# A transformer block on one core: batch passes replaced by a 16-slot pipeline, Q and K stacked by 24 transfers per group

## What is computed

```python
def attn(x, Wqkv, Wo):              # H = 16 heads of HD = 32
    q, k, v = heads(x @ Wqkv)
    scores = einsum('bhqd,bhkd->bhqk', q, k) * HD ** -0.5
    a = softmax(where(causal, scores, -1e9))
    return merge(einsum('bhqk,bhkd->bhqd', a, v)) @ Wo

def ffn(x, w1, w3, w2):             # HIDDEN = 1365
    w1q, w3q, w2q = [clip(round(w / mean(abs(w))), -1, 1) * mean(abs(w)) for w in (w1, w3, w2)]
    return (silu(x @ w1q.T) * (x @ w3q.T)) @ w2q.T

x = x + attn(layernorm(x), Wqkv, Wo)
x = x + ffn(layernorm(x), w1, w3, w2)
```

## Time and profile before

| | |
|---|---|
| time, median of 3 runs | 727.8 us (727.48 to 729.08) |
| span of the profiled execution, first to last instruction | 727.0 us |
| TensorE (PE) busy | 630.4 us, 87% |
| TensorE weight loads | 300.6 us, 41% |
| VectorE (DVE) busy | 436.0 us, 60% |
| ScalarE (ACT) busy | 335.2 us, 46% |
| GpSimd (POOL) busy | 136.4 us, 19% |
| mean granted TensorE clock | 0.941 of full speed |
| chain that ended last | PE 64%, DVE 17%, ACT 11%, issue 5% |

### The profile page before, as it was taken

How to read it: one execution, slowest core, us unless ns; L and a number is a source line. 1 busy time by engine, 2 the same in 40 slices (tenths; PEclk the granted TensorE clock), 3 DMA queues, 4 the chain that set the end, 5 groups by cost and what they waited for, 6 DMA issues and landing times.

```text
span 727.0 us, 10700 instructions
## 1 busy us (share of the span) xinstructions
PE 630.4 (87%) x3892; PEld 300.6 (41%) x3892; DVE 436.0 (60%) x816; ACT 335.2 (46%) x551; POOL 136.4 (19%) x205
## 2 busy tenths in 40 slices
PE   2695687677988999999979999999979999997998
PEld 1142333333444444444444444444434544443443
DVE  7767767974655668634575777535556775244431
ACT  2556756852345585511456555501557645202330
POOL 2000012311100233410001225401002233211330
PEclk9997888667999999999999999999999999997999
DMA  8061121300020000011100000021000000120001
GB/s 330 16 227 58 48 79 54 116 1 1 1 73 16 16 16 1 1 59 60 52 23 17 16 16 1 1 76 40 15 16 16 1 16 1 44 72 1 0 1 59
DMA packets 13930, 30.22 MB, mean 42 GB/s; under 512 B 2442, under 2 KB 2442, under 8 KB 13876
## 3 DMA queue, kind: packets, MB, share of 16 engines
q1 hardware_dynamic: 13876, 29.50, 12.8%
HBM read 20.97 MB, written 4.19 MB: 35 GB/s over the span
## 4 chain that ended last, share of the span: by engine, by line
PE 64%; DVE 17%; ACT 11%; issue 5%; DMA 2%; SPq 0%; POOL 0%; DVEq 0%; ACTq 0%; POOLq 0%
PE work L999 25%; PE work L1139 11%; PE work L1030 10%; PE sum_bank L1102 6%; PE o_bank L1102 4%; PE prob_bank L1083 3%; PE score_bank L1056 3%; ACT k_stack L625 3%; DVE block_max L829 3%; ACT probs L642 2%; DVE inv_sum L844 1%; ACT late L684 1%; DMA late<-in_L_ffn_w 1%; ACT late L657 1%; ACT q_stack L625 1%
## 5 line engine op out<-in xcount | busy, mean ns | idle before, releaser
L999 PE MATMUL work<-late,w_ternary 128*128 128x512 f16 (+1 forms) x704 | 168.3, 390 | 9.6 <-DVE late L864 8.1
L829 DVE TENSOR_REDUCE block_max<-score_bank 128x4 f32<-128x512 f32 x160 | 102.8, 684 | 52.3 <-PE score_bank L1058 52.2
L999 PEld LDWEIGHTS work<-late,w_ternary 128*128 128x128 f16 (+1 forms) x704 | 69.9, 102 | 90.6 <-DVE late L864 14.2
L642 ACT ACTIVATE probs<-prob_bank,scalars 128x512 f32<-128x512 f32 x160 | 100.6, 681 | 7.0 <-PE prob_bank L1083 6.0
L568 POOL TENSOR_TENSOR late<-late 128x512 f16<-128x512 f32 (+1 forms) x44 | 51.0, 1159 | 208.5 <-ACT late L663 208.5
L1139 PE MATMUL work<-w_ternary,late 128*128 128x512 f16 (+1 forms) x352 | 77.2, 379 | 0.0
L864 DVE SCALAR_TENSOR_TENSOR late<-late,work 128x512 f32<-128x512 f32 (+1 forms) x44 | 30.3, 688 | 68.7 <-ACT late L657 68.4
L1056 PE MATMUL score_bank<-k_stack,q_stack 96*128 96x512 f16 (+3 forms) x256 | 62.7, 310 | 9.3 <-DVE block_max L829 8.4
L844 DVE RECIPROCAL inv_sum<-sum_bank 128x512 f32<-128x512 f32 x16 | 53.7, 3358 | 21.5 <-PE sum_bank L1102 21.5
L1030 PE MATMUL work<-xt_hi,wqkv_hi 128*128 128x512 f16 x128 | 51.5, 402 | 17.0 <-DVE wqkv_lo L778 10.4
L647 ACT ACTIVATE ot_hi<-o_sb 128x512 f16<-128x512 f32 x16 | 10.1, 630 | 121.0 <-DVE o_sb L850 121.0
(11 more groups left out here) (104 smaller groups left out, 911.3 us busy)
## 6 DMA issues: line engine op xcount, KB each, us to landing
late<-in_L_ffn_w SPq DMA_DIRECT2D x6, 768.0 KB, 6.5
x_res<-in_L_attn_x SPq DMA_DIRECT2D x16, 256.0 KB, 2.7
out_y<-x_res SPq DMA_DIRECT2D x16, 256.0 KB, 2.0
late<-in_L_attn_Wqkv SPq DMA_DIRECT2D x4, 768.0 KB, 8.9
xn<-in_L_attn_x SPq DMA_DIRECT2D x3, 1024.0 KB, 5.3
late<-in_L_ffn_w SPq DMA_DIRECT2D x4, 682.5 KB, 3.9
q_stack<-q_stack SPq DMA_DIRECT2D x16, 128.0 KB, 2.3
k_stack<-k_stack SPq DMA_DIRECT2D x16, 128.0 KB, 2.3
```

The source lines that it names most:

```text
L642: act.activation(probs[:, u, :], prob_bank[u % 2][:], ACT.Exp, scale=scalar(exp_scale)).then_inc(prob_free, 1)
L829: dve.tensor_reduce(block_max[:, u, :], score_bank[u % 2][:].rearrange("p (k c) -> p k c", c=P), AX_X, ALU.max).then_inc(score_free, 1)
L999: last = pe.matmul(bank, lhs, rhs, start=(n == 0), stop=(n == len(terms) - 1))
```

## The change

The passes and the loop are gone. `order` now makes one list for all 16 groups (4 batches x 4), and each group is a slot. In slot `s` the probabilities of group `s` are computed, the scores of group `s + 1`, Q and K of group `s + 2`, and the values and sums of group `s - 1`. The remaining work is dealt over the slot's anchors by weights (`spread`): in batch 0 the weight preparation, 14 items a slot; later in a batch's four slots V with the projection of the batch before, the first 10 FFN steps, the last 12, and the down products. The turning of the next x lies in the second slot. Values and sums no longer have banks of their own, and there are four `work` banks in place of two.

Moved, added and removed per group:

- Placing: the copies on ScalarE (8) and VectorE (8) go; SyncE issues 12 transfers for Q and 12 for K from the f16 halves, 32 partitions of 1 KB each. `q_hi` and its three fellows are single buffers: ScalarE waits for the stack of the group before to be whole before it writes the next.
- Mask: the 16 mask matmuls go. VectorE adds an f32 mask and takes the maximum in one operation for each tile, 16 instead of 10 reductions and 4 small ones.
- Sums: GpSimd adds the probabilities of a head's key blocks (6 additions a group), and the sum on TensorE takes 8 matmuls, 4 of 128 and 4 of 384 columns, in place of 32.
- In batch 0 the rounding of the weights goes from VectorE to GpSimd, the splitting of Wqkv is by columns (9 pieces) instead of by rows (4).
- The next x is loaded in 4 transfers instead of 1.

The diff, cut to its core:

```diff
+def slot(s, early, late):
+
+    front = [[("scores", s + 1, 0)], [("scores", s + 1, 1)]] if s + 1 < SLOTS else [[]]
+    o = spread(front, early)
+    if s:
+        o += [("values", s - 1), ("sums", s - 1)]
+    back = []
+    for p in range(PIECES):
+        back.append([("probs", s, p)])
+        if s + 1 < SLOTS and p + 2 < PIECES:
+            back.append([("scores", s + 1, p + 2)])
+        if s + 1 < SLOTS and p == 3:
+            back.append([("max_row", s + 1)])
+    return o + spread(back, late)
...
+        early, late = qk(s + 2), []
+        if b == 0:
+            late += prep[g * n:(g + 1) * n]
+        elif g == 0:
+            late += [(2.5, [("v", b, i)]) for i in range(2)]
+            late += [(2.5, [("project", b - 1, i), ("stats_y", b - 1, i)]) for i in range(ST)]
+            late += [(2.5, [("v", b, 2), ("norm_y", b - 1, 0)]), (0.4, [("yt", b - 1, 0), ("norm_y", b - 1, 1)]),
+                     (2.5, [("v", b, 3)]), (0.4, [("yt", b - 1, 1), ("norm_y", b - 1, 2)]),
+                     (0.4, [("yt", b - 1, 2), ("norm_y", b - 1, 3)]), (0.4, [("yt", b - 1, 3)])]
+            ups = ffn_up(b - 1)
+        elif g == 1:
+            late += ups[:10]
+        elif g == 2:
+            late += ups[10:]
+        else:
+            downs = 2 if b == BATCHES - 1 else ST
+            late += [(4.7, [("down", b - 1, i)] + ([("res_load", b, i - 1)] if i else [])) for i in range(downs)]
+            late.append((0.0, [("res_load", b, downs - 1)]))
+        if g == 1 and b + 1 < BATCHES:
+            late = merged(late, next_x(b + 1))
...
-            def stack(ps, g):
-
-                i = stack_of[g]
-                wait(hi_placed, count(ps.att, 2 * GROUPS, 2 * g + 2))
-                wait(lo_placed, count(ps.att, 2 * GROUPS, 2 * g + 2))
-                sp.dma_start(q_stack[i][2 * HD:3 * HD, :, :], q_stack[i][0:HD, :, :]).then_inc(stacked[g], 16)
-                sp.dma_start(k_stack[i][HD:2 * HD, :, :], k_stack[i][0:HD, :, :]).then_inc(stacked[g], 16)
...
+            def place(step):
+
+                n, s = step
+                dst = (q_stack if n == "q" else k_stack)[s % STACKS]
+                emptied(sp, step)
+                if s >= STACKS:
+                    sp.wait_ge(prob_full, NU * (s - STACKS + 1))
+                elif n == "k":
+                    sp.wait_ge(unit_rows_set, s + 1)
+                for j, part_ in enumerate(STACK_ROWS[n]):
+                    for h in range(HG):
+                        sp.dma_start(dst[j * HD:(j + 1) * HD, h, :],
+                                     half[n, part_][h * HD:(h + 1) * HD, :]).then_inc(stacked[n][s % STACKS], 16)
...
+                pool.wait_ge(selected, SELECTS * s + 3 * (pair + 1))
+                sums = added[:, 2 * pair:2 * pair + 2, :]
+                n = ADDS * s + 3 * pair
+                pool.tensor_tensor(sums, probs[:, u:u + 4:3, P:S], probs[:, u + 1:u + 5:3, 0:S - P],
+                                   ALU.add).then_inc(added_done, 1)
+                pool.wait_ge(added_done, n + 1)
+                pool.tensor_tensor(sums[:, :, P:3 * P], sums[:, :, P:3 * P],
+                                   probs[:, u + 2, :].rearrange("p (h c) -> p h c", h=2), ALU.add).then_inc(added_done, 1)
+                pool.wait_ge(added_done, n + 2)
+                pool.tensor_tensor(sums[:, :, 2 * P:3 * P], sums[:, :, 2 * P:3 * P],
+                                   probs[:, u + 1:u + 5:3, S - P:S], ALU.add).then_inc(added_done, 1)
...
+            def weight_round(m, c):
+                if c == 0:
+                    pool.wait_ge(inv_made, WEIGHTS.index(m) + 1)
+                rows = HLAST if m != "w2" and c == HC - 1 else P
+                src = chunk_views(m, c)[0][0:rows]
+                pool.tensor_scalar(src, src, scalars[0:rows, inv_s[m]:inv_s[m] + 1], ROUND, ALU.mult,
+                                   ALU.add).then_inc(rounded, 1)
...
-            def place(ps, step):
-                g = step[1]
-                act.wait_ge(work_half, ps.half(step))
-                dst = (q_stack if step[0] == "q" else k_stack)[stack_of[g]]
-                for h in range(HG):
-                    last = act.activation(dst[0:HD, h, :], half_hi[HD * h:HD * (h + 1), :], ACT.Copy)
-                last.then_inc(hi_placed, 1)
...
+            def qk_high(step):
+                n, s = step
+                if s:
+                    act.wait_ge(stacked[n][(s - 1) % STACKS], 16 * 3 * HG * ((s - 1) // STACKS + 1))
+                full(act, step)
+                act.activation(half[n, "hi"][:], work[bank_of(step)][:], ACT.Copy, scale=QK_SHRINK).then_inc(half_done, 1)
...
-                for h in range(HG):
-                    last = dve.tensor_copy(dst[lo_row:lo_row + HD, h, :], half_lo[HD * h:HD * (h + 1), :])
-                last.then_inc(lo_placed, 1)
...
+            def maxima(s, p):
+
+                if s == 0 and p == 0:
+                    dve.wait_ge(mask_made, 1)
                 for u in (2 * p, 2 * p + 1):
-                    dve.wait_ge(score_full, count(ps.att, NU * GROUPS, NU * g + u + 1))
-                    dve.tensor_reduce(block_max[:, u, :], score_bank[u % 2][:].rearrange("p (k c) -> p k c", c=P),
-                                      AX_X, ALU.max).then_inc(score_free, 1)
-                if p < PIECES - 1:
-                    return
-                dve.wait_ge(score_free, count(ps.att, NU * GROUPS, NU * (g + 1)))
-                bm = block_max[:].rearrange("p (a r) k -> p a r k", a=2)
-                nm = neg_max[:].rearrange("p (a h) t -> p a h t", a=2)
-                dve.tensor_reduce(nm[:, :, :, 3], bm[:, :, 0:4:3, :], AX_X, ALU.max, negate=True).then_inc(max_ready, 1)
-                dve.tensor_reduce(nm[:, :, :, 2], bm[:, :, 1:5:3, 0:3], AX_X, ALU.max, negate=True).then_inc(max_ready, 1)
-                dve.tensor_reduce(nm[:, :, :, 1], bm[:, :, 2, :].rearrange("p a (h k) -> p a h k", h=2),
-                                  AX_X, ALU.max, negate=True).then_inc(max_ready, 1)
-                dve.tensor_scalar(nm[:, :, :, 0], bm[:, :, 1:5:3, 3], -1.0, None, ALU.mult).then_inc(max_ready, 1)
...
+                    dve.wait_ge(score_full, NU * s + u + 1)
+                    for j, (h, tile, off, n) in enumerate(UNITS[u]):
+                        k = NP * s + BEFORE[u] + j
+                        if k > 1:
+                            dve.wait_ge(score_free, k - 1)
+                        dve.tensor_tensor_reduce(masked[:, k % 2, 0:n], score_bank[u % 2][:, off:off + n],
+                                                 mask[:, S - n:S], 1.0, LOWEST, ALU.add, ALU.max,
+                                                 row_max[:, h, tile:tile + 1]).then_inc(score_free, 1)
...
+                before = ("values", s)
+                bank = bank_of(before)
+                full(dve, before)
+                dve.tensor_tensor(o_sb[:], work[bank][:], o_sb[:], ALU.mult).then_inc(work_free[bank], 1)
...
-                        pe.matmul(bank[:, off:off + n], q[0:3 * HD, h, tile * P:(tile + 1) * P],
-                                  k[0:3 * HD, h, 0:n], start=True, stop=False)
-                        last = pe.matmul(bank[:, off + n - P:off + n], mask_rows[:], mask_cols[:],
-                                         start=False, stop=True)
+                        last = pe.matmul(score_bank[u % 2][:, off:off + n], q[0:3 * HD, h, tile * P:(tile + 1) * P],
+                                         k[0:3 * HD, h, 0:n], start=True, stop=True)
...
+                pe.wait_ge(added_done, ADDS * (s + 1))
+                for cols in (slice(0, P), slice(P, S)):
+                    for h in range(HG):
+                        src = probs[:, 5 * (h // 2) + 3 * (h % 2), cols] if cols.start == 0 else added[:, h, :]
+                        last = pe.matmul(work[bank][HD * h:HD * (h + 1), cols], ones[:], src,
+                                         start=True, stop=True, skip_group_check=True)
+                last.then_inc(work_full[bank], 1)
```

1146 lines of the change are left out of this document (537 added, 609 removed).

## The result

The changed kernel takes **779.6 us** (median of 4 runs, 778.9 to 780.5), against 728.0 in runs of the kernel before on the same chip: a ratio of 1.070, 95% interval 1.068 to 1.072. It is slower by 7%, where 681 us was forecast. The span of its profiled execution is 778.7 us. TensorE is busy 602.6 us of it (before 630.4), VectorE 386.4 (436.0), ScalarE 254.8 (335.2), GpSimd 284.5 (136.4). Three of the engines have less to do, as forecast, and the kernel is longer.

The account below looks back on a forecast made before the run. TensorE was taken to bound the middle passes, waits between engines batch 0. Start 66, batch 0 112, batches 1 and 2 285.2, batch 3 122.1, rest 95.1: 680.4, with 0.8 for the median 681 us; range 652 to 712.

Parts of the forecast that it names:

- Batch 0, slots of 28 us (112 together): Four slots with weight preparation: 28 us each, 2 us of it stall; bounds 24.5 and 35; slot 4 at 178.
- lower bound of 24.5: Batch 0's slots: ScalarE's chain with nothing waiting, 24.5 us a slot.
- Another engine binds: Rival: masked maxima cost twice as much, or GpSimd's additions bring batch 0's slots to 35; about 710 us, chance 0.19.
- GpSimd busy over 80% in batch 0: Batch 0: one of the signs that would show the forecast wrong.
- The start, slot 0 at 66: Time before slot 0, with nothing covering the transfers: slot 0 starts at about 66 us, a gain of 2.
- Batches 1 and 2, gaps of 6.5 us: Batches 1 and 2: TensorE's work 136 us plus gaps of 6.5, down from 12, so 142.6 each.
- Batch 3 and the tail: Batch 3 to slot 15: 122.1 us with 10 of gaps; the rest 95.1, with an unchanged tail of 81.4.
- Fewer gaps: Rival: batch 0's slots at ScalarE's 24.5 us, a batch's gaps 2 to 3; about 653 us, chance 0.14.
- no overlap: Rival: gaps stay at 12 us, batch 0's slots at 30; about 700 us, no chance of its own.
- TensorE's terms: Per group: mask matmuls save 0.9 us, sums 1.4; a group costs 12.6 and a batch 136.
- SyncE, 0.56 us an issue and hidden in the middle: Placing Q and K: 24 transfers a group, 13.4 us of issues, costing nothing in the middle slots.
- The transfers bind: Rival: SyncE's transfers set the slot, above 1.4 us each; slower than before, 737 to over 1000 us, chance 0.05.

Follow-up runs that it names:

- e2: Changed kernel with the weights' cross-partition totals on TensorE and one tiny GpSimd addition after its last cross-partition maximum: 753.7 us.
- e1: Changed kernel with the 33 roundings of the FFN weights back on VectorE: 755.0 us.
- e12: Kernel before, with only the roundings of the FFN weights moved to GpSimd: 741.3 us, ratio 1.017.
- e3: Changed kernel with the loads of w3 and w2 issued by ScalarE instead of SyncE: 770.9 us.
- e13: Changed kernel with e1, e2, e3, e4, e9, e6 (outside first slots), k_stack fills later, next x's normalisation out of second slots: 679.0 us, ratio 0.933.
- e14: e13 with the roundings back on GpSimd: 686.2 us.
- e4: Changed kernel with the scaling and splitting of Wo moved earlier, between Q and K of group 1: 774.4 us.
- e9: Changed kernel with four tiles for the normalised y instead of two, each normalisation right behind the next projection: 759.8 us.
- e6: Changed kernel with the f16 halves of o made behind a slot's second pair of exponents instead of at its front: 778.4 us.
- e16: e13 with the softmax sums in 32 matmuls a group and no additions on GpSimd: 691.9 us.
- e8: Changed kernel with 16 more transfers a group from group 6 on, into rows that nothing reads: 793.6 us.

## Why the prediction was wrong

**Batch 0, slots of 28 us (112 together): the step that failed.** They took 174.0. The prediction counted 2 us of stall a slot, from additions ahead of a rounding. What it missed stands in the trace of before: reductions across partitions are on the same engine, and there are pauses around them without a releaser, as here in GpSimd's timeline from 140 to 165 us:

```profile
150.98 0.44 POOL L536 PARTITION_ALL_REDUCE scalars<-scalars  x1 [6.01 <-issue]
158.22 1.39 POOL L563 TENSOR_TENSOR ot_lo<-o_sb,ot_hi 128x512 f16<-128x512 f32 x1 [6.79 <-issue]
```

It read durations of GpSimd's operations and not the idle time in front of them, which cost little as long as the roundings were on VectorE. e2 shows the change-over as the cause of some 26 us of the changed kernel; e1 (24.6) and e12 (14.5 in the kernel before, with the move of the roundings in it) agree. e3 shows 8.7 us for the weight loads: the prediction put the 24 issues ahead of the row maxima and not ahead of the loads. The four slots are 120.4 us in e13, 8 over the forecast, and its upper bound of 35 a slot lay under the 43 of the result. Its lower bound of 24.5, by ScalarE's chain, doesn't follow from its own terms either: 9 and 17 are 26.

**"Another engine binds", about 710:** the right place and engine, with the wrong mechanism and a price far too low. It had the additions ahead of the roundings, which e14 puts at no more than 7 us, and not the change-overs. TensorE was busy 51% of the time, the others less; it was a chain of waits. The sign of "GpSimd busy over 80% in batch 0" was the wrong one: it was 37%, 65.0 of 174.

**The start, slot 0 at 66:** 71.2. VectorE waited 3.8 us for GpSimd's first reduction, which stood behind a pause of 7.3, and e4 found 5 us in Wo.

**Batches 1 and 2, gaps of 6.5 us:** 152.3 a batch in place of 142.6. The sum for TensorE, 136, is near what e13 shows (133.6 busy in 136.1). The term that was mis-sized is the gaps: 7 to 8 us by two y tiles where the kernel before had four, which the prediction did not price, and the second slot, named as "the one place where VectorE nearly binds", was 40.6 against 34.

**Batch 3 and the tail:** by the forecast's boundary slots 12 to 15 took 135.3 for 122.1, and the rest 93.7 for 95.1. e9 gives 6.7 of the 13 back by the y tiles and e6 7.0 in the last slot, where the halves of o stood ahead of the exponents.

**The other rivals.** "Fewer gaps" (653) and "no overlap" (about 700) fell with the same slots.

**TensorE's terms.** The sums at 1.4 a group were right (1.3 in e16). No run undoes the masking, so its 0.9 stays unpriced by itself. The masked maxima were dearer in the forecast than in the trace, 10.3 against 111.9 / 16 = 7.0 us a group:

```profile
L785 DVE CUSTOM_DVE_ANT_0 masked<-score_bank,mask 128x512 f16<-128x512 f32 x64 | 44.0, 687 | 0.9 <-PE score_bank L982 0.6 <-issue 0.3
...
L785 DVE DVE_READ_ACCUMULATOR2_ANT row_max<- 128x1 f32 x256 | 21.3, 83 | 0.0
...
L528 POOL TENSOR_TENSOR added<-probs 128x768 f32<-128x768 f32 x32 | 58.3, 1822 | 17.2 <-issue 14.7
...
L557 POOL TENSOR_SCALAR late<-late,scalars 128x512 f32<-128x512 f32 x30 | 20.3, 691 | 6.9 <-issue 6.9
```

**SyncE, 0.56 us an issue and hidden in the middle:** 0.62 (2.49 for four), and hidden, as e8 needed 16 more issues a group to make it show. "The transfers bind" is wrong.

The Trainium skill (DMA: Bandwidth & Descriptors, Anatomy of one DMA) has a fixed 2.0 us a transfer, fitted to transfers that GpSimd issues; here SyncE issues them. These landed 1.8 to 1.9 us after their issue and overlapped, so the estimate of 50 us a slot by that figure does not hold.

What stays open: 8 us of batch 0 in e13 over the forecast, the 3.2 us later start of e9, and what the moved mask is worth by itself.

## What to carry to other kernels

Before a step moves to another engine, read on that engine the idle time in front of its operations, "issue" above all, and not only their durations: a pause that hurt nobody becomes part of the chain once something waits behind it. A pipeline that changes many things at once can hide its gains: the transfers were worth 4 us with the other waits in place and 16 without them, and the whole went from 7% slower to 7% faster by eight small edits. When a rewrite halves a buffer, price the wait of whoever writes the third tile.

## What the runs showed of the hardware

- GpSimd paused between the cross-partition reduction and tensor-tensor or tensor-scalar arithmetic, in both directions: 5.8 to 7.5 us in the changed kernel's slots (five pauses), 6.0 and 6.8 in the kernel before, up to 9.8 in e1. The triangular selection behind a reduction started after 0.16 us (e12).
- Two pauses of 2.8 and 2.7 us in an otherwise full stretch were followed by the lower level of TensorE's clock for some 5.5 us (512 columns in 0.43 us instead of 0.22), which by difference cost 2.4 us more; in e9, without the pauses, the clock stayed at the upper level.
- A dozen SBUF-to-SBUF transfers of 32 KB in a row issue every 0.62 us and land in 1.8 to 1.9, so they overlap.
